# TensorE's expert loop: the turning back of the outputs moved ahead of the jump to the expert's code, and skipped before the first expert

## The chip, the cores and the metric

The kernel runs on one core of a Trainium2 chip. The metric is the device time of one launch in microseconds (us); less is better. The engines are called TensorE (PE in the profile, PEld its weight loads, PEldq what its sequencer does by itself: register operations, branches, waits), VectorE (DVE), ScalarE (ACT), GpSimd (POOL) and SyncE (SP, which issues DMAs).

## The reference, cut to what matters

A block of three parts on 2 x 1024 tokens of width 512: a mixture of experts, a gated mixer with a cumulative sum and a short convolution, and the same mixture of experts again. The change lies in the two mixtures.

```python
x = x + 0.5 * ffn(layernorm(x), gate_weight, wi, wo)
x = x + attn(layernorm(x), ...)
x = x + 0.5 * ffn(layernorm(x), gate_weight, wi, wo)

def ffn(inputs, gate_weight, wi, wo):        # 8 experts, 320 places each
    ...                                      # softmax, top 1, rank inside the expert
    dispatch = jnp.einsum('tec,th->ech', sec_mask, tokens)
    hmid = jax.nn.gelu(jnp.einsum('ech,ehi->eci', dispatch, wi), approximate=False)
    eout = jnp.einsum('eci,eih->ech', hmid, wo)
    return jnp.einsum('tec,ech->th', combine_weights, eout)
```

## The kernel before, in words

Each mixture (a `Layer`, n = 0 and 1) first computes where every token goes. Then the eight experts are worked through one after the other. Every matrix product is made of three: operands are split into a high and a low part in fp32r, and `product` and `onto` issue high x high, high x low and low x high (lines 1184 to 1186 and 1191 to 1193).

For an expert e TensorE first transposes its gathered and normalized tokens `dn`: `turn_tokens` (line 1355) is 12 transposes into four PSUM banks, `acc0`, `acc1`, `psH1` and `psH0`. ScalarE copies each bank to `dth`, VectorE subtracts and gives `dtl` (line 763), and counts `dt_lo` once for each of the four. The product with wi (`mm1`) goes into `psH`, the one with wo (`mm2`) is summed over the whole expert in the four banks `acc`. Those are cleared before by `clear_acc`, four tiny matmuls (line 1361), for which the third `dtl` must be there (`dt_lo` at 4e + 3), since the banks `acc0` and `acc1`, and `psH1` for what comes behind, hold turned tokens until then.

The output of an expert, `eoT` (copied by ScalarE from `acc`, line 660), is transposed back one expert later: `turn_out` (line 1399) turns 128 + 128 of its 320 columns into `psT0` and `psT1`, eight transposes, and `turn_rest` (line 1406) the last 64 into `psH1`, four transposes. VectorE then scales and adds to `rows` (line 1043), and GpSimd scatters these to memory. Before the first expert of a layer both functions run on an `eoT` that holds nothing of use, and their counts keep the semaphores in step. `eoT` is set to zero once by VectorE at the very start (line 917).

Of the kernel before, what the change touches and what calls it, by code (L numbers as in the profile page):

```python
# [32 lines left out]
DC = D // P  # L33
E, INTER = 8, 2048
# [45 lines left out]
def build_kernel(nc, x, wuT, wvT, wg1T, wg2T, small_in, wi, wo, out):  # L80
# [6 lines left out]
    with ExitStack() as ctx:  # L87
# [12 lines left out]
        def put(name, shape, dt):  # L100
            t = at(name, shape, dt, top[0])
            top[0] += size(shape, dt)
            return t
# [59 lines left out]
        eoT = put("eoT", [P, DC, CAP], F32)  # L163
# [586 lines left out]
        def _(dve):  # L750
            seq = [0]

            def then(ins):

                ins.then_inc(dve_seq, 1)
                seq[0] += 1
# [157 lines left out]
            for bank in (*acc[2:], *psH):  # L914
                ins = dve.memset(bank[:, 0:CAP], 0.0)
            ins.then_inc(banks_set, 1)
            then(dve.memset(eoT[:, :, :], 0.0))
            then(dve.memset(gates[:, :, :], 0.0))
            for e in range(E):
                then(dve.memset(digit[:, e:e + 1], float(2 ** (CODE * e))))  # L920
# [7 lines left out]
            for n, s in enumerate(layers):  # L928
# [28 lines left out]
                def wi_split(e, step, s=s):  # L957
                    k = (step // 2) % 2
                    dve.wait_ge(s.wi_hi, STEPS * e + step + 1)
                    lo(wil[:, step % 2, :, :], raw_wi[k][:, :, (step % 2) * HALF:(step % 2 + 1) * HALF],  # L960
                       wih[:, step % 2, :, :]).then_inc(s.wi_lo, 1)

                def wo_split(e, step, s=s):
                    k = (step // 2) % 2
                    dve.wait_ge(s.wo_hi, STEPS * e + step + 1)
                    lo(wol[:, step % 2, :, :], raw_wo[k][:, (step % 2) * ICS:(step % 2 + 1) * ICS, :],
                       woh[:, step % 2, :, :]).then_inc(s.wo_lo, 1)

                def tokens(e, c, s=s):

                    dve.wait_ge(s.dt_hi, DC * e + c + 1)
                    lo(dtl[:, c, :], TURNED[c][:, 0:CAP], dth[:, c, :]).then_inc(s.dt_lo, 1)
# [3 lines left out]
                def stage(e, h, a, sources, s=s, base=base):  # L976

                    for k in range(CHUNKS):
                        dve.wait_ge(gathered[1 - a][k], base + 16 * h + 16 * a + 16)
                    q = bass.ds(CHUNKS * e + CHUNKS, CHUNKS)  # L980
                    dve.tensor_copy(dst_now[:, 1 - a, :], dst[:, q])
                    dve.tensor_copy(facts_now[:, 1 - a], table[:, q, :]).then_inc(s.now_set, 1)  # L982
                    if sources:
                        dve.tensor_copy(src_now[:, a, :], src[:, bass.ds(CHUNKS * e + 2 * CHUNKS, CHUNKS)]
                                        ).then_inc(s.src_set, 1)
# [7 lines left out]
                def hidden_split(e, step, s=s):  # L993

                    k = step % 2
                    dve.wait_ge(s.gelu_done, ICS + ICS * (STEPS * e + step + 1))
                    if k == 0:
                        dve.wait_ge(s.mm2a_done, PAIRS * e + step // 2 + 1)
                    else:
                        dve.wait_ge(s.acc_done, DC * (PAIRS * e + step // 2 + 1))  # L1000
                    dve.tensor_copy(hth[:, k, :, :], gel[:, k, :, :]).then_inc(s.ht_hi, 1)  # L1001
                    dve.wait_ge(s.ht_hi, STEPS * e + step + 1)
                    lo(htl[:, k, :, :], gel[:, k, :, :], hth[:, k, :, :]).then_inc(s.ht_lo, 1)

                def mixer_weights(i):

                    if i == 0:
                        dve.wait_ge(g_hi, 2)
                        lo(wg1[1][:, :, :], raw_g1[:, :, :], wg1[0][:, :, :]).then_inc(g_lo, 1)
                        lo(wg2[1][:, :], raw_g2[:, :], wg2[0][:, :]).then_inc(g_lo, 1)  # L1010
                    for step in (2 * i, 2 * i + 1):
                        k, c = divmod(step, DC)
                        dve.wait_ge(uv_hi, step + 1)
                        w = (wu, wv)[k]
                        lo(w[1][:, c, :], raw_u[k][:, c, :], w[0][:, c, :]).then_inc(uv_lo, 1)

                def expert(h, side, last, sources, s=s):
                    e = 2 * h + side
                    for i in range(PAIRS):
                        a, b = 2 * i, 2 * i + 1  # L1020
                        wo_split(e, b)
                        hidden_split(e, a)
                        if not last or a + 2 < STEPS:
                            wi_split(e, a + 2)
                        hidden_split(e, b)
                        if not last or b + 2 < STEPS:
                            wi_split(e, b + 2)
                        if i == 1 and not last:
                            stage(e, h, side, sources)
                        if last and s is layers[0]:  # L1030
                            mixer_weights(i)
                        if not last or a + 2 < STEPS:
                            wo_split(e, a + 2)

                    if not last:
                        for c in range(DC):
                            tokens(e + 1, c)
                    dve.wait_ge(s.now_set, e + 1)
                    for i, (k, bank) in enumerate(HELD):
                        m = ROWS[k]  # L1040
                        dve.wait_ge(s.outT_done, e + 2)
                        out_rows = rows[side][0:m, k, :]
                        dve.scalar_tensor_tensor(out_rows, bank[0:m, :], facts_now[0:m, side, k, WEIGHT:WEIGHT + 1],  # L1043
                                                 out_rows, ALU.mult, ALU.add).then_inc(s.out_dve, 1)
# [93 lines left out]
                for g in range(GROUPS):  # L1138
                    more = g + 1 < GROUPS
# [40 lines left out]
        def _(pe):  # L1180
# [23 lines left out]

            codes = pe.alloc_register("codes")
            width = pe.alloc_register("width")
            visits = [[], []]
            marks = []
            pe.wait_ge(pool_const, 3)
# [9 lines left out]
            for n, s in enumerate(layers):  # L1219
# [138 lines left out]
                def clear_acc():  # L1358

                    for c in range(DC):  # L1360
                        pe.matmul(acc[c][:, 510:512], ones[:, :], ones[:, 0:2], start=True, stop=True)
# [27 lines left out]
                    if k == 0:  # L1389
                        ins.then_inc(s.mm2a_done, 1)  # L1390

                def turn_out(e, s=s):

                    pe.wait_ge(s.out_dve, 3 * e)
                    for c in range(DC):
                        pe.wait_ge(s.eoT_done, DC * e + c + 1)
                        for k, bank in HELD[1:]:
                            q, m = k * P, ROWS[k]
                            pe.transpose(bank[0:m, c * P:(c + 1) * P], eoT[:, c, q:q + m], ident[:, :])  # L1399

                def turn_rest(s=s):

                    k, bank = HELD[0]
                    q, m = k * P, ROWS[k]
                    for c in range(DC):
                        ins = pe.transpose(bank[0:m, c * P:(c + 1) * P], eoT[:, c, q:q + m], ident[:, :])
                    ins.then_inc(s.outT_done, 1)

                def expert(e, w, s=s):
                    pe.wait_ge(s.dt_lo, DC * e + 3)  # L1410
                    clear_acc()
                    turn_rest()
                    with pe.Fori(0, PAIRS) as i:
                        mm1(e, 2 * i, 0, w)
                        mm1(e, 2 * i + 1, 1, w)
                        mm2(e, 2 * i, 0, w)
                        mm2(e, 2 * i + 1, 1, w)
# [12 lines left out]
                pe.wait_ge(s.taken_done, 1)  # L1430
                pe.reg_load(codes, code[0:1, 0:1])
                pe.wait_ge(s.wi_lo, 1)
                pe.addr_align(BLOCK, offset=BLOCK - 2, max_nops=0)
                with pe.Fori(0, E) as e:
                    pe.wait_ge(s.dn_done, CHUNKS * e + CHUNKS)
                    for c in range(DC):
                        if c < 2:
                            pe.wait_ge(s.eoT_done, DC * e + c + 1)
                        turn_tokens(e, c)
                    turn_out(e)  # L1440
                    pe.reg_alu(width, codes, 2 ** CODE - 1, ALU.bitwise_and)
                    pe.reg_alu(codes, codes, CODE, ALU.logical_shift_right)
                    head = nc.cur_bb
                    dispatch("run")
                    nc.switch_bb(f"join_{n}", parent=head)
                    pe.addr_align(BLOCK, offset=BLOCK - 3, max_nops=0)
# [7 lines left out]
                        pe.addr_align(BLOCK, offset=BLOCK - 1, max_nops=0)  # L1454
                        pe.br(f"visited_{w}_{n}")
                nc.switch_bb(f"done_{n}", parent=over_bb)
                turn_out(E)
                turn_rest()

                if n == 1:  # L1460
                    break
# [72 lines left out]
                for g in range(GROUPS):  # L1534
                    more = g + 1 < GROUPS
# [89 lines left out]
```

## Time and profile before

| | |
|---|---|
| time, median of 3 runs | 1121.2 us (1119.05 to 1122.02) |
| the profiled execution's own time | 1119.05 us |
| its span, first to last instruction | 1117.3 us |
| TensorE's mean granted clock in it | 0.966 of full |
| TensorE matmul busy | 1049.7 us (94%) |
| VectorE busy | 722.1 us (65%) |
| ScalarE busy | 545.4 us (49%) |
| GpSimd busy | 148.0 us (13%) |

A boundary between two experts is the stretch from the last `mm2` matmul of one to the first `mm1` matmul of the next. There are 14 of them, seven in each layer, and two starts of a layer. They are called here by the expert that begins: 1 to 7 of the first layer, 1 to 7 of the second, and expert 0 for a start. The widths, by the shapes of line 1184, are 288, 304, 272, 240, 288, 240, 240, 256 in the first layer and 320, 240, 240, 240, 240, 240, 320, 320 in the second.

### The profile page before, as it was taken

How to read it: one execution, taken by the hardware profiler on the slowest of the kernel's cores; microseconds unless marked ns; L12 is line 12 of the kernel's file. 1: busy time of each engine (PE TensorE's matmuls, PEld its weight loads, DVE VectorE, ACT ScalarE, POOL GpSimd, SP SyncE). 2: the span in 40 equal slices, each digit the busy share in tenths (PEclk: the TensorE clock that was granted, in tenths of full speed). 3: DMA queues.
4: the chain of work that ended last, by engine and by line, in shares of the span. 5: the costliest groups of instructions: out<-in, count | busy, mean ns of one | idle time of the engine just before them, and what ended most of it. 6: DMA issues, size and time to landing. Idle time of an engine off the chain costs nothing.

```text
span 1117.3 us, 20930 instructions
## 1 busy us (share of the span) xinstructions
PE 1049.7 (94%) x7898; PEld 996.1 (89%) x7898; DVE 722.1 (65%) x1089; ACT 545.4 (49%) x853; POOL 148.0 (13%) x135
## 2 busy tenths in 40 slices
PE   8599999999999999399999995999999999999995
PEld 6599999999999999377777774999999999999995
DVE  7466556666676777378776774557767677665652
ACT  5345445655556565254243223445656656554441
POOL 2201102113020210100000013002112021130101
PEclk9599999999999999699999996999999999999998
DMA  8368636475555651400011017445475565654400
GB/s 304 103 253 297 229 114 230 146 254 195 195 202 188 239 187 63 165 10 1 1 39 37 2 49 269 156 143 211 177 250 212 204 215 195 233 203 149 171 38 24
DMA packets 83283, 177.43 MB, mean 159 GB/s; under 512 B 4192, under 2 KB 4704, under 8 KB 83168
## 3 DMA queue, kind: packets, MB, share of 16 engines
q1 hardware_dynamic: 75776, 153.13, 38.7%
q0 software_dynamic: 7168, 23.07, 5.7%
q8 instruction: 34, 0.56, 0.2%
q10 hardware_dynamic: 288, 0.52, 0.1%
q14 instruction: 17, 0.14, 0.0%
HBM read 162.04 MB, written 18.87 MB: 162 GB/s over the span
## 4 chain that ended last, share of the span: by engine, by line
PE 90%; DMA 2%; issue 2%; DVE 2%; ACT 1%; POOL 1%; POOLq 0%; SPq 0%; DVEq 0%; ACTq 0%
PE psH L1184 12%; PE psH L1186 12%; PE psH L1185 12%; PE acc L1193 11%; PE acc L1191 11%; PE acc L1192 11%; PE acc L1184 3%; PE acc L1186 3%; PE acc L1185 3%; PE psT L1399 1%; PE psT L1235 1%; PE psH L1307 1%; PE acc L1355 1%; PE psH L1355 1%; DMA rows<-out_x,src_now 1%
## 5 line engine op out<-in xcount | busy, mean ns | idle before, releaser
L1184 PE MATMUL psH<-dth,wih 128*128 128x240 f32 (+5 forms) x1024 | 295.4, 288 | 0.1
L1186 PE MATMUL psH<-dth,wil 128*128 128x240 f32 (+5 forms) x1024 | 294.2, 287 | 0.0
L1185 PE MATMUL psH<-dtl,wih 128*128 128x240 f32 (+5 forms) x1024 | 293.9, 287 | 0.0
L1193 PE MATMUL acc<-hth,wol 128*128 128x240 f32 (+5 forms) x1024 | 293.5, 287 | 0.0
L1191 PE MATMUL acc<-hth,woh 128*128 128x240 f32 (+5 forms) x1024 | 293.2, 286 | 0.0
L1192 PE MATMUL acc<-htl,woh 128*128 128x240 f32 (+5 forms) x1024 | 293.2, 286 | 0.0
L763 DVE TENSOR_TENSOR wol<-raw_wo,woh 128x1024 fp32r<-128x1024 f32 x128 | 155.6, 1222 | 140.3 <-ACT woh L594 140.3
L628 ACT ACTIVATE gel<-psH 128x320 f32<-128x320 f32 x256 | 111.8, 437 | 188.7 <-PE psH L1186 183.4
L594 ACT ACTIVATE woh<-raw_wo 128x1024 fp32r<-128x1024 f32 x128 | 134.2, 1056 | 126.4 <-PE acc L1193 126.4
L1184 PEld LDWEIGHTS psH<-dth,wih 128*128 128x128 f32 x1024 | 193.7, 189 | 0.6 <-ACT gel L628 0.2
L1186 PEld LDWEIGHTS psH<-dth,wil 128*128 128x128 f32 x1024 | 193.7, 189 | 0.0
L1185 PEld LDWEIGHTS psH<-dtl,wih 128*128 128x128 f32 x1024 | 193.7, 189 | 0.0
L1193 PEld LDWEIGHTS acc<-hth,wol 128*128 128x128 f32 x1024 | 193.0, 188 | 0.0
L1191 PEld LDWEIGHTS acc<-hth,woh 128*128 128x128 f32 x1024 | 193.0, 188 | 0.0
L1192 PEld LDWEIGHTS acc<-htl,woh 128*128 128x128 f32 x1024 | 193.0, 188 | 0.0
L763 DVE TENSOR_TENSOR wil<-raw_wi,wih 128x1024 fp32r<-128x1024 f32 x128 | 155.8, 1219 | 0.1
L583 ACT ACTIVATE wih<-raw_wi 128x1024 fp32r<-128x1024 f32 x128 | 134.6, 1053 | 1.4 <-DMA raw_wi<-in_wi 1.3
L1001 DVE CAST hth<-gel 128x640 fp32r<-128x640 f32 x128 | 63.3, 494 | 93.0 <-ACT gel L628 92.5
L763 DVE TENSOR_TENSOR htl<-gel,hth 128x640 fp32r<-128x640 f32 x128 | 105.7, 826 | 4.4
L498 POOL DMA_INDIRECT out_x<-rows,dst_now x24 | 35.7, 1488 | 326.2 <-DVE rows L1043 321.4
L498 POOL DMA_INDIRECT x<-rows,dst_now x24 | 35.3, 1470 | 322.3 <-DVE rows L1043 317.4
L611 ACT ACTIVATE dn<-rows,facts_now 128x512 f32<-128x512 f32 x48 | 38.9, 810 | 63.6 <-DVE facts_now L982 37.4
(189 smaller groups left out, 1158.6 us busy)
## 6 DMA issues: line engine op xcount, KB each, us to landing
raw_wi<-in_wi SPq DMA_DIRECT2D x64, 1024.0 KB, 5.1
raw_wo<-in_wo SPq DMA_DIRECT2D x64, 1024.0 KB, 5.4
out_x<-xt SPq DMA_DIRECT2D x4, 1024.0 KB, 5.1
xt<-in_x SPq DMA_DIRECT2D x6, 512.0 KB, 8.2
xt<-x SPq DMA_DIRECT2D x3, 1024.0 KB, 9.7
raw_u<-in_wuT SPq DMA_DIRECT2D x1, 1024.0 KB, 10.3
raw_u<-in_wvT SPq DMA_DIRECT2D x1, 1024.0 KB, 12.4
xt<-x SPq DMA_DIRECT2D x4, 256.0 KB, 3.4
```

Of the source, the lines that this page charges most:

```text
L498: pool.indirect_dma_start(target[:, :], bass.IndirectOffsetOnAxis(ap=dst_now[0:m, a, k:k + 1], axis=0), rows[a][0:m, k, :], None).then_inc ...
L583: act.activation(wih[:, step % 2, :, :], raw_wi[k][:, :, (step % 2) * HALF:(step % 2 + 1) * HALF], copy).then_inc(s.wi_hi, 1)
L594: act.activation(woh[:, step % 2, :, :], raw_wo[k][:, (step % 2) * ICS:(step % 2 + 1) * ICS, :], copy).then_inc(s.wo_hi, 1)
L628: act.activation(gel[:, step % 2, j, :], psH[j][:, 0:CAP], ACT.Gelu).then_inc(s.gelu_done, 1)
L763: return dve.tensor_tensor(out, full, hi.bitcast(F32), ALU.subtract)
L1001: dve.tensor_copy(hth[:, k, :, :], gel[:, k, :, :]).then_inc(s.ht_hi, 1)
L1184: pe.matmul(out, lh, rh, start=first, stop=False)
L1185: pe.matmul(out, lh, rl, start=False, stop=False)
L1186: return pe.matmul(out, ll, rh, start=False, stop=last)
L1191: pe.matmul(out, lh, rh, start=False, stop=False, skip_group_check=True)
L1192: pe.matmul(out, lh, rl, start=False, stop=False, skip_group_check=True)
L1193: return pe.matmul(out, ll, rh, start=False, stop=False, skip_group_check=True)
```

## The change

It does four things. (1) `clear_acc` and `turn_rest` leave the code of the widths and stand in the loop over e, behind the eight transposes of `turn_out` and ahead of the two register operations and the ladder. The wait for the third `dtl` moves with them. (2) A new register, `later`, is 0 for expert 0 and 1 behind it. With 0 the loop only waits for the third `dtl` and clears the banks: none of the 12 transposes of `eoT` is made, and `outT_done` isn't counted. With 1 it does what the kernel before did. (3) VectorE waits for `outT_done` one lower, since it counts one fewer. (4) The setting of `eoT` to zero goes.

```diff
-            then(dve.memset(eoT[:, :, :], 0.0))
...
-                        dve.wait_ge(s.outT_done, e + 2)
+                        dve.wait_ge(s.outT_done, e + 1)
...
+            later = pe.alloc_register("later")
...
-                def turn_out(e, s=s):
+                def turn_out(e, more=True, s=s):
 
                     pe.wait_ge(s.out_dve, 3 * e)
                     for c in range(DC):
@@
                         for k, bank in HELD[1:]:
                             q, m = k * P, ROWS[k]
                             pe.transpose(bank[0:m, c * P:(c + 1) * P], eoT[:, c, q:q + m], ident[:, :])
-
-                def turn_rest(s=s):
-
+                    if more:
+                        pe.wait_ge(s.dt_lo, DC * e + 3)
+                        clear_acc()
                     k, bank = HELD[0]
                     q, m = k * P, ROWS[k]
                     for c in range(DC):
                         ins = pe.transpose(bank[0:m, c * P:(c + 1) * P], eoT[:, c, q:q + m], ident[:, :])
                     ins.then_inc(s.outT_done, 1)
 
-                def expert(e, w, s=s):
-                    pe.wait_ge(s.dt_lo, DC * e + 3)
-                    clear_acc()
-                    turn_rest()
+                def expert(e, w):
                     with pe.Fori(0, PAIRS) as i:
...
+                pe.reg_mov(later, 0)
                 pe.addr_align(BLOCK, offset=BLOCK - 2, max_nops=0)
                 with pe.Fori(0, E) as e:
...
-                    turn_out(e)
+                    with pe.If_lt(later, 1):
+                        pe.wait_ge(s.dt_lo, 3)
+                        clear_acc()
+                    with pe.Else():
+                        turn_out(e)
+                    pe.reg_mov(later, 1)
                     pe.reg_alu(width, codes, 2 ** CODE - 1, ALU.bitwise_and)
                     pe.reg_alu(codes, codes, CODE, ALU.logical_shift_right)
...
-                turn_out(E)
-                turn_rest()
+                turn_out(E, False)
```

## Rows read from the trace of the kernel before

**Rows 1.** The page: TensorE's busy time, and the chain's shares.

```profile
PE 1049.7 (94%) x7898; PEld 996.1 (89%) x7898; DVE 722.1 (65%) x1089; ACT 545.4 (49%) x853; POOL 148.0 (13%) x135
...
PE 90%; DMA 2%; issue 2%; DVE 2%; ACT 1%; POOL 1%; POOLq 0%; SPq 0%; DVEq 0%; ACTq 0%
```

**Rows 2.** Timeline at expert 1, first layer: start us, us, engine, line, count, [idle before].

```profile
104.42 0.88 DVE L763 TENSOR_TENSOR dtl<-psH,dth 128x320 fp32r<-128x320 f32 x2
104.95 0.17 PEld L1361 LDWEIGHTS acc<-ones 128*128 128x128 bf16 x4 [0.23 <-DVE dtl L763]
...
105.43 0.19 PEld L1184 LDWEIGHTS psH<-dth,wih 128*128 128x128 f32 x1
```

**Rows 3.** Sequencer by line, experts 0 and 1: ns min/median/max, first and last start.

```profile
L1413 PEldq MOVE  x1: 34/34/34, 50.5 to 50.5; - x1
...
L1441 PEldq ALU_OP  x1: 36/36/36, 103.3 to 103.3; - x1
L1426 PEldq COMPARE_BRANCH  x5: 64/69/207, 103.5 to 104.1; - x5
L1413 PEldq MOVE  x1: 29/29/29, 105.0 to 105.0; - x1
```

**Rows 4.** Sequencer by line: ladders of 240, 288, 320 and 272 columns.

```profile
L1426 PEldq COMPARE_BRANCH  x1: 213/213/213, 313.8 to 313.8; - x1
L1441 PEldq ALU_OP  x1: 36/36/36, 313.6 to 313.6; - x1
...
L1426 PEldq COMPARE_BRANCH  x4: 64/76/331, 260.3 to 260.8; - x4
...
L1441 PEldq ALU_OP  x1: 36/36/36, 984.7 to 984.7; - x1
L1428 PEldq COMPARE_BRANCH  x1: 169/169/169, 985.6 to 985.6; - x1
...
L1426 PEldq COMPARE_BRANCH  x3: 69/82/3562, 159.3 to 159.6; - x3
```

**Rows 5.** Timeline at expert 2, first layer: VectorE's last two dtl, and TensorE.

```profile
160.25 0.88 DVE L763 TENSOR_TENSOR dtl<-psH,dth 128x320 fp32r<-128x320 f32 x2
163.26 0.17 PEld L1361 LDWEIGHTS acc<-ones 128*128 128x128 bf16 x4 [2.71 <-issue]
```

**Rows 6.** Windows: from:to us, length, busy by engine (x count), PEclk granted clock, DMA.

```profile
47.20:51.40 4.20, 4.17 (x20) 4.17 (x21) 1.97 (x4) 2.62 (x6) 2.84 (x3) 0.50 0.91 320
163.50:167.00 3.50, 3.50 (x20) 3.47 (x19) 2.97 (x4) 0.40 (x1) 1.41 (x1) 0.58 0.02 5
472.50:478.00 5.50, 5.47 (x20) 4.52 (x21) 2.08 (x3) 4.23 (x8) 0.00 (x0) 0.50 0.58 220
478.00:481.50 3.50, 2.11 (x9) 1.29 (x7) 1.29 (x3) 1.69 (x3) 0.00 (x0) 0.98 0.00 0
672.50:676.00 3.50, 2.06 (x40) 1.86 (x41) 2.44 (x17) 1.51 (x2) 0.00 (x0) 1.00 0.99 316
```

**Rows 7.** Timeline at expert 0 of the first layer.

```profile
49.63 1.72 PEld L1399 LDWEIGHTS psT<-ident,eoT 128*128 128x128 f32 x8
...
49.92 1.13 DVE L763 TENSOR_TENSOR dtl<-psH,dth 128x320 fp32r<-128x320 f32 x2
...
51.34 0.32 PEld L1361 LDWEIGHTS acc<-ones 128*128 128x128 bf16 x4
...
51.95 0.19 PEld L1184 LDWEIGHTS psH<-dth,wih 128*128 128x128 f32 x1
```

**Rows 8.** Timeline at expert 0 of the second layer: the third dtl, and the first mm1.

```profile
695.89 0.49 DVE L763 TENSOR_TENSOR dtl<-psH,dth 128x320 fp32r<-128x320 f32 x1
...
697.50 0.19 PEld L1184 LDWEIGHTS psH<-dth,wih 128*128 128x128 f32 x1
```

**Rows 9.** Timeline of VectorE at the kernel's start.

```profile
2.55 1.12 DVE L917 MEMSET eoT<- 128x1280 f32 x1 [0.26 <-issue]
...
5.73 0.19 DVE L924 TENSOR_TENSOR gates<-small,acc 128x32 f32<-128x32 f32 x1 [1.79 <-PE acc L1216]
```

## The prediction

> **What bounds the kernel now.** I read the page first. TensorE's matmuls are busy for 1049.7 of the span's 1117.3 us, and the chain of work that ended last lies on TensorE for 90% [rows 1]. So whatever holds TensorE up at an expert's boundary is paid in full, and whatever another engine saves there is worth nothing by itself. Next I read the timeline at each boundary, because the change lies there alone. At expert 1 the eight transposes of `turn_out` are done, TensorE is idle for 0.23 us for the third `dtl`, then clears, turns the rest, and loads the first weights of `mm1` at 105.43 [rows 2]. The other warm boundaries look the same to within 0.02 us, except expert 2.
>
> The timeline shows no branches, so the third view is the sequencer's own instructions, line by line. At expert 1 the first register operation of the ladder starts at 103.3, its five comparisons run from 103.5 to 104.1 and the last takes 0.21; then nothing until the `MOVE` that opens the inner loop, at 105.0 [rows 3]. The third `dtl` ends at 104.42 + 0.49 = 104.91 (one of them takes 0.49 [rows 8]; the two of the row overlap). So the ladder is free today: it runs while the sequencer would otherwise wait for `dtl`. And the sequencer stands at that wait; it doesn't run on past it. Expert 0 shows this best: the third `dtl` ends at 49.92 + 0.49 = 50.41, the `MOVE` comes at 50.5 [rows 3], although TensorE only reaches the clearing at 51.34 [rows 7]. Three times the `MOVE` follows the third `dtl` by about 0.08 us. From the `MOVE` to the first weight load of `mm1` are 0.45 us (105.0 to 105.43) of register operations and waits; the array needs about as long for clearing and turning (104.95 to 105.43). The boundary is therefore balanced: anything put on the sequencer behind the wait comes out at `mm1`.
>
> **The change, part by part.** The wait for the third `dtl` now stands ahead of the ladder. Behind it, one after the other, come: the pushes of 8 instructions (inside the 0.08 us), `reg_mov`, the two register operations, the ladder, the inner loop's opening, `mm1`.
>
> *The ladder, 14 boundaries.* Its price is from the start of line 1441 to the end of the last branch [rows 4]. For 240 columns 313.8 + 0.21 - 313.6 = 0.41; for 288 260.8 + 0.33 - 260.3 = 0.83 and the 0.2 of the two register operations ahead of it (103.3 to 103.5), 1.03; for 304 104.1 + 0.21 - 103.3 = 1.01 [rows 3]; for 320 985.6 + 0.17 - 984.7 = 1.07. For 272, 159.6 - 159.1 = 0.5 up to the jump and a normal jump of 0.21, so 0.7; for 256 I take 0.7 too, between 240 and 288 and near 272. Seven boundaries in the first layer: 1.01 + 0.7 + 0.41 + 1.03 + 0.41 + 0.41 + 0.7 = 4.7. In the second five of 240 and two of 320: 2.05 + 2.14 = 4.2. A last jump can take 0.33 instead of 0.21, as at 288; for others like it I allow 0.3 more. Together 9.2 us. Of this nothing is hidden, by the balance above; at most the 0.02 us of slack.
>
> The Trainium skill ("Advanced Engine Details and Errata", Control Flow Timing) puts a compare-and-branch at about 108 ns and an unconditional one at about 51 ns. By it the 32 comparisons behind these 14 boundaries and two jumps would be an estimated 3.6 us, and with the two register operations unpriced the ladder would come out far cheaper; the trace has steps of 0.12 to 0.2 and a last jump of 0.21 to 0.35, and it decides.
>
> *`reg_mov` and the joint.* A register operation takes a step of 0.1 us (line 1441 to the first comparison is 0.2 for two [rows 3]), and a branch leaves about 0.03 before the next: 14 x 0.13 = 1.8.
>
> *The end of the Else part.* It may need a jump to where both parts meet. The trace has none; the nearest row is line 1428 with 0.17 [rows 4]. So 0 to 14 x 0.17 = 2.4; I take the middle, 1.2. The comparison for `later` is ahead of `turn_out`, where the sequencer waits for ScalarE's last `eoT` anyway: nothing.
>
> *Expert 0, without the transposes.* TensorE saves 12 transposes in each layer, some 2 us of a slow clock in the first. But `mm1` can't start before the sequencer's chain is through: third `dtl` 50.41 + 0.08 + 0.1 + ladder 0.9 + 0.03 + 0.45 = 51.97, against 51.95 today [rows 7]: nothing. In the second layer (320 columns) 696.38 + 0.08 + 0.1 + 1.07 + 0.03 + 0.45 = 698.1, against 697.50 [rows 8]: 0.6 lost. With the joint's jump 0.2 more for both. Bounds: 0.4 and 1.2.
>
> *The clock at expert 0.* TensorE comes to each layer's first expert at the lower level, 1.2 GHz: from 47.2 to 51.4 it works without a break at a granted 0.50, and then the clock is full, just before `mm1` starts [rows 6]. The transposes that the change takes out are the second half of that work. Without them TensorE works from 47.2 to about 49.8, is idle for 2 us, and the heavy matmuls start cold. How long they stay so: the stretch of unbroken work ahead of the rise was 4.2 us here and 5.5 us at 472.5 to 478 [rows 6]. Half of it is lost, 2.1 to 2.8; it was 3.4 us behind expert 2's gap (0.58 granted over 3.5 us), 1.7. I take 1.9 for each layer, 3.8 together; bounds 0 (the clock rises in spite of the gap) and 5.6.
>
> *Expert 2 of the first layer.* Its ladder's last jump took 3.56 us: the code for 272 wasn't there and was fetched. 1.15 us of that is hidden today, since the jump starts at 159.6 and the third `dtl` is ready at 160.25 + 0.49 = 160.74; the rest is in the idle 2.71 [rows 4, 5]. Afterwards the jump starts at 160.74 + 0.08 + 0.1 + 0.5 = 161.4 and ends at 165.0, where it ends by 163.26 today: 1.7, of which 0.8 is counted in the ladder and joint, so 0.9 more. The clock fell behind that gap and was half for some 3.4 us; behind one of 3.9 it may stay so for as long again: 0 to 1.7, I take 0.9.
>
> *The clock at the other boundaries.* Each gets an idle gap of 0.5 to 1.2 us beside today's 0.23. With 2.11 of 3.5 us busy the clock stayed full at 478, and with 2.06 it fell behind 676 [rows 6]; a boundary for 304 or 320 columns leaves about as much. A fall costs 1.7. Four boundaries are that wide: 0 to 6.8, and I take 0.5, as all but the widest stay well above.
>
> *VectorE's memset.* 1.12 us are gone, but VectorE then waits 1.79 us for TensorE's first product [rows 9]: nothing; with less than that wait it would be worth its 1.12 at most. VectorE's wait for `outT_done` one lower is the same event as before, and its adding to `rows` is hidden behind `mm1` as now.
>
> Sum: 9.2 + 1.8 + 1.2 + 0.6 + 0.2 + 3.8 + 0.9 + 0.9 + 0.5 = 19.1 us. On the profiled execution's own 1119.05 (its span of 1117.3 and 1.75 around it) that is 1138.2. The median of the runs shown lies 2.15 higher; I add part of that and say 1139.
>
> **The rivals.** (a) *The sequencer isn't held.* If a waiting transpose is handed to the array's queue and the sequencer goes on, the ladder stays hidden. Then only expert 0 changes: `mm1` follows the fourth `dtl` (49.92 + 1.13 = 51.05, and 0.1 [rows 7]), 0.8 earlier in the first layer and at most as much in the second, and without or with the 3.8 of the clock the time is 1117.5 to 1121.3: no change. It decides if at every boundary the first branch of line 1426 starts ahead of the third `dtl`. Against it speaks that the `MOVE` comes behind the wait at all boundaries. The Trainium skill ("Perfetto Trace Analysis", per-instruction lifecycle) says for TensorE just what this rival needs: the wait is served in a queue behind the sequencer, which is ready for the next instruction after the push. By that rule the trace would have the `MOVE` of expert 1 near 104.4; it has it at 105.0 [rows 3]. 6 in 100.
>
> (b) *The fetch of expert 2 goes away.* The loop's code gets longer and the widths' shorter, and which blocks are at hand could change. But both still fit in a block each, and the order in which blocks are entered is the same. Then expert 2 saves 1.7 instead of losing 1.7, and 2.6 of clock: 1138.2 - 6.0 = 1132. 10 in 100.
>
> (c) *More falls of the clock or more fetches.* A fetch costs 3.4 and its fall of the clock 1.7; two of them, or six falls beyond those counted, give 1148; a fall at all 14 boundaries 1160. For it: the boundaries come close to the stretch behind which the clock fell. Against: TensorE worked through 478 to 481.5 with as much idle time at full clock. 8 in 100.
>
> My forecast, then, has 76 in 100.
>
> **How the numbers follow.** The likeliest is 1139. With the low ends of the unknown costs (no joint's jump, no loss of clock at expert 0) it is 1119.05 + 9.2 + 1.8 + 0.4 + 0.9 = 1131.4; with the high ones (2.4, 1.2, 5.6, 1.7, 3.4) 1119.05 + 9.2 + 1.8 + 2.4 + 1.2 + 5.6 + 0.9 + 1.7 + 3.4 = 1145.3, and 2 more for the median. With (b) and most of (c) the range is 1130 to 1148. About 0.3% is what a measurement of this kernel can tell from no change. Faster needs both (a) and (b): 2 in 100. Within 0.3% is the rest of (a): 4. Slower is all else: 94.
>
> **What would show it.** In the profile of the changed kernel the ladder's first branch should start about 0.3 us behind the third `dtl`, and `mm1`'s first weight load about 1.0 us behind it for 240 columns and 1.7 for 320, where it is 0.53 now. TensorE should show a new idle gap at each boundary behind the rest's transposes, put down to issue. The clock should be half for some us behind the start of `mm1` in both first experts. The long jump should stand at expert 2 again. Wrong would be the prediction if those gaps are missing (a), if the long jump is gone or is there more than once (b, c), or if the second layer's 240s lose more than the ladder's 0.41 and about 0.2.

## The result

The changed kernel takes 1138.18 us (median; 1137.5 to 1140.88), the kernel before 1121.2 us (1119.05 to 1122.02). The ratio is 1.0157, with a 95% interval of 1.0142 to 1.0174: slower by 17 us. The profiled execution took 1136.17 us, with a span of 1134.3, against 1119.05 and 1117.3 before. The forecast was 1139 in a range of 1130 to 1148. All ratios here are of fast executions; of all executions below two were slow, one of 5902.66 us (the filler) and one of 2693.16 us (the second entry into the code).

The page of the changed kernel, its span, TensorE's time and the chain's shares, beside [rows 1]:

```profile
span 1134.3 us, 20909 instructions
...
PE 1053.2 (93%) x7874; PEld 995.7 (88%) x7874; DVE 721.8 (64%) x1088; ACT 545.7 (48%) x853; POOL 147.5 (13%) x135
...
PE 89%; issue 3%; DMA 2%; DVE 2%; ACT 2%; POOL 1%; POOLq 0%; SPq 0%; DVEq 0%; ACTq 0%
```

TensorE makes 24 matmuls fewer (the 12 transposes of each layer's expert 0) and is none the less busy for 3.5 us longer, which is the clock; "issue" in the chain has gone from 2% to 3%. The list of TensorE's waits names the place (waiter, what released it: us in total, times, longest):

```profile
PE psH L1183 <- issue: 14.5, 16, 3.8
```

Sixteen waits, one for each expert, ahead of the first `mm1` matmul, released by nothing but the sequencer. The kernel before has no such row. Line 1183 is `product`'s first matmul, 1184 before: most lines on TensorE stand one to three higher or lower now.

The timeline at expert 1 of the first layer, beside [rows 2]:

```profile
105.57 0.91 PEld L1399 LDWEIGHTS psT<-ident,eoT 128*128 128x128 f32 x8
...
106.17 0.88 DVE L763 TENSOR_TENSOR dtl<-psH,dth 128x320 fp32r<-128x320 f32 x2
...
106.70 0.17 PEld L1361 LDWEIGHTS acc<-ones 128*128 128x128 bf16 x4 [0.23 <-DVE dtl L763]
...
106.80 0.36 PEld L1406 LDWEIGHTS psH<-ident,eoT 128*64 128x64 f32 x4
...
108.25 0.19 PEld L1183 LDWEIGHTS psH<-dth,wih 128*128 128x128 f32 x1 [1.09 <-issue]
```

And the sequencer's own instructions there, beside [rows 3]:

```profile
L1443 PEldq MOVE  x1: 29/29/29, 106.7 to 106.7; - x1
...
L1444 PEldq ALU_OP  x1: 36/36/36, 106.8 to 106.8; - x1
...
L1423 PEldq COMPARE_BRANCH  x5: 64/69/207, 107.0 to 107.5; - x5
...
L1410 PEldq MOVE  x1: 29/29/29, 107.8 to 107.8; - x1
```

Up to the clearing nothing has moved: it comes 2.47 us behind the first transpose of tokens in both kernels (104.24 to 106.70 here), with the same 0.23 us of waiting for the third `dtl`. Then the old order was clearing, `MOVE` of the inner loop, `mm1`; the new one has the move of `later` (106.7), two register operations, five comparisons and only then the loop's `MOVE` at 107.8. TensorE's weight loads for the four transposes are over by 107.16, and the weight-load side is idle for 1.09 us; on the matmul side, where the sum of 14.5 us is taken, the gap is 0.83.

The distance from the first weight load of `turn_tokens` (line 1355) to the first one of `mm1`, read from the two timelines, in us:

| expert | 0 | 1 | 2 | 3 | 4 | 5 | 6 | 7 |
|---|---|---|---|---|---|---|---|---|
| layer 1, columns | 288 | 304 | 272 | 240 | 288 | 240 | 240 | 256 |
| before | 4.72 | 2.94 | 5.44 | 2.93 | 2.90 | 2.94 | 2.90 | 2.90 |
| after | 5.24 | 4.01 | 7.01 | 3.62 | 4.04 | 3.52 | 3.50 | 3.72 |
| layer 2, columns | 320 | 240 | 240 | 240 | 240 | 240 | 320 | 320 |
| before | 4.30 | 2.96 | 2.91 | 2.90 | 2.90 | 2.90 | 2.90 | 2.96 |
| after | 5.37 | 3.66 | 3.47 | 3.50 | 3.51 | 3.47 | 4.09 | 4.12 |

The 14 boundaries grew by 11.8 us, the two starts by 1.6. Behind the starts the first expert itself took 1.5 us longer in the first layer and 2.6 in the second, at the same number of matmuls. That is 17.6; the rest of the span gave back 0.6 (0.3 ahead of the first expert and 0.7 in the mixer gained, 0.4 lost inside the other experts), which makes the 17.0 between the spans.

The 1.5 and 2.6 are the clock, as windows of the changed kernel show (columns as in [rows 6]; the granted clock is the third number from the end):

```profile
49.80:51.90 2.10, 0.25 (x4) 0.16 (x4) 1.50 (x3) 2.10 (x3) 0.69 (x1) 1.00 1.00 381
...
53.20:56.60 3.40, 3.40 (x17) 3.40 (x16) 0.35 (x1) 0.44 (x1) 0.00 (x0) 0.50 0.46 166
...
700.80:706.00 5.20, 3.08 (x16) 2.61 (x16) 2.88 (x5) 3.64 (x6) 2.83 (x3) 0.50 0.93 317
706.10:712.10 6.00, 5.92 (x22) 5.93 (x23) 1.34 (x2) 0.44 (x1) 0.00 (x0) 0.51 0.66 201
```

In the first layer the clock had just risen, TensorE did almost nothing for 2.1 us, and the clock fell again for 3.4 us in the middle of `mm1`. In the second it never rose ahead of `mm1` and stayed at 1.2 GHz for the first 6 us of it.

### The profile page after: what moved, and what is told of

The parts are those of the page before. It is cut to its first block, busy times and chain, and to the rows that moved or that the text cites. A ratio compares the mean times of both kernels' runs of the same rounds, so it can differ in the third digit from the quotient of the medians.

```text
span 1134.3 us, 20909 instructions
## 1 busy us (share of the span) xinstructions
PE 1053.2 (93%) x7874; PEld 995.7 (88%) x7874; DVE 721.8 (64%) x1088; ACT 545.7 (48%) x853; POOL 147.5 (13%) x135
## 4 chain that ended last, share of the span: by engine, by line
PE 89%; issue 3%; DMA 2%; DVE 2%; ACT 2%; POOL 1%; POOLq 0%; SPq 0%; DVEq 0%; ACTq 0%
PE psH L1183 13%; PE psH L1184 12%; PE psH L1185 12%; PE acc L1191 11%; PE acc L1192 11%; PE acc L1190 11%; PE acc L1183 3%; PE acc L1184 3%; PE acc L1185 3%; PE psT L1235 1%; PE psT L1399 1%; PE psH L1307 1%; PE acc L1355 1%; PE psH L1355 1%; DMA rows<-out_x,src_now 1%
## 5 line engine op out<-in xcount | busy, mean ns | idle before, releaser
L1183 PE MATMUL psH<-dth,wih 128*128 128x240 f32 (+5 forms) x1024 | 297.4, 290 | 15.2 <-issue 14.5
```

Of the source, the lines that this page charges most:

```text
L1183: pe.matmul(out, lh, rh, start=first, stop=False)
```

## The experiments

They ran on three chips, four on each; which chip the first comparison ran on isn't known. There the kernel before took 1125.9 to 1128.3 us and scattered more. So two things are read: the ratio to the kernel before on the same chip, and, from one profiled execution of each kernel, the distances at the boundaries, which hardly differ from chip to chip. No profile of the kernel before was taken on these chips; where its behaviour there is spoken of, it is read from kernels that keep its boundaries.

**Hoisting alone.** The changed kernel without `later`, without If and Else and with the memset back.

```diff
-                    with pe.If_lt(later, 1):
-                        pe.wait_ge(s.dt_lo, 3)
-                        clear_acc()
-                    with pe.Else():
-                        turn_out(e)
-                    pe.reg_mov(later, 1)
+                    turn_out(e)
```

> One half of the change alone: clearing and the last four transposes stand ahead of the ladder at every expert, and nothing is skipped at expert 0 (no register later). Theory (the sequencer is held at the wait for the third dtl, so what stands behind it is paid in full): the 14 boundaries cost what the changed kernel's cost, 11.8 us, less a register move of 0.1 each, so 10.4; expert 0 costs 0 in the first layer and 0.5 in the second, and its clock rises ahead of mm1 as in the kernel before. Together 10.9 us, 1132 us. Rival (the loss comes from the skipping at expert 0 and its If and Else): no change, 1121 us.

The distances at the 14 boundaries grew by 10.55 us in all, at expert 0 by 0.09 and 0.69, and both first experts ran as fast as before: the distances are the expected ones to 0.2. The ratio is not: 1.0052 (1.0034 to 1.007), 1134.75 against 1128.28 us, some 6 us where 11 were due. The list of TensorE's waits has both the price and what came off:

```profile
PE psH L1184 <- issue: 10.3, 15, 4.0
...
PE psH L1184 <- ACT gel L628: 1.5, 2, 0.9
```

The second row, waits for gelu, is not in the list of the kernel before on the first chip. What it means came out of the next runs.

**Skipping alone**, on the kernel before: the eight transposes of `turn_out` are left out at expert 0, all else stays.

```diff
-                    turn_out(e)
+                    with pe.If_lt(first, 1):
+                        turn_out(e)
+                    pe.reg_mov(first, 0)
                     pe.reg_alu(width, codes, 2 ** CODE - 1, ALU.bitwise_and)
```

> The other half alone, on the kernel before: the eight transposes of turn_out are left out at expert 0, all else stays where it was (the last four transposes are still made at expert 0, and the ladder stays ahead of the wait). Theory: mm1 of expert 0 then follows the fourth dtl, 0.8 us earlier in the first layer and 0.35 in the second, but its matmuls run at the lower clock for some us, which costs 2 to 4.2; the 14 boundaries are unchanged. Together 1 to 3 us slower, 1122 to 1124 us, and the granted clock is half for some us behind the start of mm1 in both layers. Rival (the clock doesn't hang on these transposes): 1.2 us faster, 1120 us.

1126.39 against 1128.28 us, ratio 0.9984 (0.9967 to 1.0001). `mm1` of expert 0 came 0.82 and 0.31 us earlier, as expected, and 13 of the 14 boundaries stayed within 0.01 (expert 2, with the fetch, came 0.32 later). The clock cost little here: it rose to full at 50.3 us in the first layer, just as `mm1` started and TensorE had no gap behind it, and 1.3 us behind the start of `mm1` in the second, where the first expert took 0.6 us longer. The window of the first 1.7 us from there, columns as above:

```profile
50.30:52.00 1.70, 1.70 (x15) 1.70 (x14) 1.25 (x2) 1.36 (x2) 0.00 (x0) 1.00 0.83 289
```

The theory's 1 to 3 us slower lie outside the interval, and what was to be lost by the clock, 2 to 4.2, was 0.6. The rival's 1.2 us faster lie inside it: with the last four transposes left in their place, the eight others were hardly missed. And the waits for gelu are there again, in the list of TensorE's waits (us in total, times, longest):

```profile
PE psH L1184 <- ACT gel L628: 7.3, 6, 1.9
```

**More sequencer work behind the wait and ahead of it.** Two pairs. In the first, four more moves of the constant into `later`, behind the wait in the changed kernel and ahead of it in the kernel before.

> The changed kernel with the register move of later made five times instead of once, behind the wait for the third dtl and ahead of the ladder. Theory: each move costs a step of 0.1 us at each of 16 experts, 4 x 16 x 0.1 = 6.4 us on top of 1138.2, so 1144.6 us. Rival (the sequencer has slack there, and the loss is the array's or the clock's): 1138 us as without.

> The kernel before with the same four register moves between turn_out and the ladder, ahead of the wait for the third dtl. Theory: the ladder ends 0.55 us or more ahead of that wait's end, and four moves are 0.4 us, so nothing: 1121 us. Rival (a register operation costs TensorE its 0.1 us wherever it stands): 6.4 us, 1127.6 us.

These tell nothing on their question: the traces show none of the added moves (16 moves of `later` in the first kernel, one for each expert, and none in the second), so they weren't in the program that ran. They are a second look at the two kernels on a slower chip: 1141.39 us (ratio 1.0111, 1.0081 to 1.0141) and 1129.71 (1.0012, 0.9995 to 1.0029). The first has the changed kernel's distances again (12.3 us more at the 14 boundaries, 0.4 of the difference at expert 2 with its fetch), but its clock cost nothing at the first start and 2.5 us at the second, where the first look had 1.5 and 2.6.

In the second pair the extra work is five waits for semaphores that were reached long ago. In the trace they are two instructions for each expert, not five, and those start 0.11 us apart.

```diff
+                    for done in (s.taken_done, s.rank_done, s.tabled, s.oh_done, s.lgT_copied):
+                        pe.wait_ge(done, 1)
                     pe.reg_alu(width, codes, 2 ** CODE - 1, ALU.bitwise_and)
```

> The changed kernel with five waits for semaphores that have long been reached put between the last four transposes and the ladder, at every expert. Theory: the sequencer serves each in 0.05 to 0.1 us and mm1 starts that much later at all 16 experts, 4 to 8 us on top of the changed kernel. Rival (the sequencer has slack there): nothing.

> The kernel before with the same five waits between turn_out and its ladder, ahead of the wait for the third dtl. Theory: the ladder of the widest code ends 0.55 us ahead of that wait's end, so the five waits are hidden at all boundaries, or cost 0.1 at those for 320 columns: nothing. Rival: the same 4 to 8 us as behind the wait.

The two instructions at expert 1, behind the wait:

```profile
L1445 PEldq EVENT_SEMAPHORE  x2: 51/51/51, 107.7 to 107.8; - x2
```

Behind the wait each distance grew by some 0.21 us over the changed kernel's (for 240 columns, at experts 2 to 5 of the second layer, 3.68 to 3.72 instead of 3.47 to 3.51; for 320 columns 4.30 instead of 4.09), and by 0.55 at expert 2, whose fetch took longer: 3.7 us over 16 experts, a little less than the 4 to 8 expected. Ahead of it 13 boundaries stayed within 0.01 us of the kernel before. Expert 2 came 0.42 later, where the fetch took 3.77 instead of 3.56 us, and the two starts 0.38 and 0.22 later, which tells nothing: over the five kernels that keep the old order and all transposes the start lies 4.1 to 5.1 us behind the first transpose in the first layer and 4.3 to 5.1 in the second. The sum of TensorE's waits for the sequencer in the first of the two went from 14.5 to:

```profile
PE psH L1183 <- issue: 18.3, 16, 4.4
```

Times: 1142.8 us (ratio 1.0127, 1.0095 to 1.0158) and 1126.41 (0.9988, 0.9969 to 1.0007). At the boundaries the same instructions are paid or free by the side of the wait on which they stand.

**Work for the clock.** The changed kernel with eight transposes of the identity at expert 0, which nothing reads.

```diff
                     with pe.If_lt(later, 1):
+                        for c in range(DC):
+                            for _, bank in HELD[1:]:
+                                pe.transpose(bank[:, c * P:(c + 1) * P], ident[:, :], ident[:, :])
                         pe.wait_ge(s.dt_lo, 3)
```

> The changed kernel, with eight transposes of the identity put back at expert 0 ahead of the clearing, as work for the array alone: nothing reads them. Theory: the start of mm1 at expert 0 stays where the changed kernel has it (5.2 and 5.4 us behind the first transpose of tokens), as the sequencer sets it, but the clock rises ahead of or shortly behind it in both layers, so that the 4.2 us that the changed kernel's profile lost there by the clock come back, or most of them: 1134 to 1136 us where the changed kernel takes 1138. Rival (the clock's fall is set by the idle time ahead of mm1 alone, which stays): as the changed kernel.

`mm1` started where the changed kernel starts it (5.22 and 5.36 us behind the first transpose, against 5.24 and 5.37), and the first experts then took 0.00 us longer than before in both layers, where the changed kernel took 1.5 and 2.6. The windows over the same stretches:

```profile
51.90:56.60 4.70, 4.08 (x34) 4.00 (x33) 2.26 (x2) 1.64 (x4) 0.00 (x0) 0.99 0.46 145
...
706.00:712.00 6.00, 5.16 (x36) 5.05 (x35) 3.12 (x4) 2.71 (x4) 0.67 (x1) 0.89 0.58 208
```

The clock is full when `mm1` starts (in the second layer it rose at 707.3, and `mm1` starts at 708.5), and stays so. So TensorE's missing work ahead of `mm1` is what the clock's loss comes from. The rival isn't settled by this, though, since the idle time didn't stay: the eight transposes fill most of it. TensorE's first weight load of `mm1` at expert 0, first in the changed kernel, then with the filler:

```profile
52.15 0.19 PEld L1183 LDWEIGHTS psH<-dth,wih 128*128 128x128 f32 x1 [1.84 <-issue]
...
52.74 0.19 PEld L1183 LDWEIGHTS psH<-dth,wih 128*128 128x128 f32 x1 [0.70 <-issue]
```

Whether the shorter gap or the longer work ahead of it keeps the clock, no run separates. And in the first layer alone the 0.00 would prove little, as the changed kernel lost nothing there either in the profile of the repeated moves; in the second it lost 1.3 to 2.6 in all its profiles. The time was 1136.07 us, ratio 1.0059 (1.0039 to 1.008). The changed kernel itself didn't run on this chip; the kernel with the five waits, less their 3.7 us, makes an estimated 1139, some 3 us more than with the filler.

**The fetch of expert 2.** The kernel before, with one more jump into each width's code meant to be made from the loop's own block, ahead of the first layer's loop.

> The kernel before, with one more jump into each of the six widths' code from the block of the loop itself, once in the first layer, while TensorE waits for the first gathered rows. Theory: the code for 272 columns is then at hand at expert 2, so its jump takes 0.2 instead of 3.6 us, mm1 starts 2.5 us earlier there, and the clock doesn't fall behind it, 1.7 us: 4.2 us faster than the kernel before, unless the jumps themselves hold up expert 0. Rival (the blocks at hand are fewer than eight, so the code is pushed out again): no change, or a second long jump elsewhere, up to 3.5 us slower.

1127.48 against 1128.03 us, ratio 0.9988 (0.9969 to 1.0006), no change. The long jump stood at expert 2 as always, the longest of the 41 branches:

```profile
L1426 PEldq COMPARE_BRANCH  x41: 64/78/3680, 48.2 to 1060.5; - x41
```

But the run tells nothing on theory and rival, because the extra jumps weren't made. The trace has not one instruction of the added lines (1435 and 1463) and 208 branches on TensorE's sequencer, just as many as the kernel before. Between the last entry into a width's code and the loop stands one branch, into the aligned block, and at once the load of `codes`. It is a further look at the kernel before, no more:

```profile
L1431 PEldq COMPARE_BRANCH  x1: 396/396/396, 45.6 to 45.6; - x1
...
L1438 PEldq TENSOR_LOAD <-code x2: 319/402/484, 46.1 to 696.5; - x2
```

Whether a second entry would keep the code for 272 columns at hand, and why it alone is gone by then, stays open.

**Where part of the loss goes on a slower chip.** The waits for gelu were 7.3, 6.4, 4.8 and 4.3 us in the four kernels above with the old boundaries (skipping alone, the repeated moves ahead, the second entry into each width's code, the waits ahead), and 1.5, 1.7, 2.0 and 1.7 in the four with the ladder behind the wait (hoisting alone, the repeated moves behind, the filler, the waits behind). Each is of one profiled execution; the first and the third of these took 4 and 7 us more than their kernel's median. At the first of those with old boundaries, ScalarE stood behind VectorE, and VectorE behind its copy for the next expert (`stage`, line 981), which waits for the gathered rows. That wait in the kernel with the repeated moves, old boundaries, on the slower chip, then in the kernel before on the first chip, then in hoisting alone:

```profile
DVE dst_now L981 <- DMA rows<-out_x,src_now: 10.5, 5, 3.4
...
DVE dst_now L981 <- DMA rows<-in_x,src_now: 7.0, 3, 2.9
```

```profile
DVE dst_now L981 <- DMA rows<-out_x,src_now: 5.6, 5, 1.4
...
DVE dst_now L981 <- DMA rows<-in_x,src_now: 2.6, 3, 0.9
```

```profile
DVE dst_now L981 <- DMA rows<-out_x,src_now: 7.6, 5, 2.3
...
DVE dst_now L981 <- DMA rows<-in_x,src_now: 2.7, 3, 1.1
```

The median gather took 5.9 and 6.3 us from issue to landing in the first of these and 5.2 and 5.3 in the second. In the third, on the same chip as the first, it was 5.0 and 5.9, and in the changed kernel in the first comparison 4.7 and 5.7: so it differs between kernels on one chip too, and not by the chip alone. The chain scatter, gather, `stage` starts when the outputs have been turned back, which the change leaves where it is; `mm1` and all behind it comes 0.6 to 1.2 us later. So the theory: a later `mm1` gives this chain room, and part of the loss pays for waits that would have come. The last four runs test that, on one chip. The move in both kernels is:

```diff
-                        if i == 1 and not last:
-                            stage(e, h, side, sources)
                         if last and s is layers[0]:
                             mixer_weights(i)
                         if not last or a + 2 < STEPS:
                             wo_split(e, a + 2)
+                        if i == 1 and not last:
+                            stage(e, h, side, sources)
```

and on ScalarE its first `norm_rows` likewise behind `wo_split(e, a + 2)`.

> The changed kernel itself, unchanged, on the chip of the next three. Theory: where the gathers and scatters of rows take longer (the kernel before takes 1128 instead of 1121 us), the kernel before loses 4 to 7 us in waits of VectorE for gathered rows, which hold up TensorE through ScalarE's gelu; the changed kernel starts mm1 later by 0.6 to 1.2 us at each boundary, while the scatter and gather start at the same time, so it loses only 1 to 2 us there. Its ratio to the kernel before is then 1.010 to 1.012 and not 1.0157. Rival (the loss is the same everywhere): 1.015 to 1.017.

> The kernel before, with VectorE's wait for the gathered rows (and ScalarE's first normalization behind it) moved behind the next split of wo, so that it stands in nobody's way some 2 us longer. Theory: TensorE's waits for gelu at the later steps go away: 4 to 6 us faster than the kernel before on a chip where that takes 1128, 0 to 1 on one where it takes 1121. Rival (the wait moves on to the normalized rows or to the next gather, or those waits have another cause): no change or slower.

> The changed kernel with the same move of VectorE's wait. Theory: it has only 1 to 2 us of such waits to lose, so it gains 1 to 2 us over the changed kernel, and stands 14 to 18 us behind the kernel before with the move: the whole price of the change is seen once nothing absorbs it. Rival: it gains as much as the kernel before does, and the distance stays as in the pair without the move.

> The kernel before with that move and with the eight transposes of turn_out left out at expert 0: the candidate that keeps what the change saves without what it costs. Theory: mm1 of expert 0 starts 0.8 and 0.3 us earlier, and the clock costs 0 to 2.6 us in each layer, by where its rise falls: between 1 us faster and 4 us slower than the kernel with the move alone. Rival: 1.1 us faster each time.

| kernel | median us | ratio to before | waits for gelu, us |
|---|---|---|---|
| changed | 1140.83 | 1.0138 (1.0119 to 1.0157) | 0.3 |
| before, late stage | 1121.33 | 0.9960 (0.9945 to 0.9974) | none |
| changed, late stage | 1137.85 | 1.0112 (1.0093 to 1.0131) | none |
| before, late stage, skipping alone | 1118.55 | 0.9945 (0.9926 to 0.9964) | 0.8 |

The kernel before took 1125.89 us on this chip. The late stage took 4.6 us off it and 3.0 off the changed kernel, and with nothing left to absorb it the price of the change is 16.5 us, where it was 14.9 without the move. What is shown is that the late stage takes time off the kernel before (its interval lies below 1) and that no wait for gelu is left with it. The rest is not: the intervals of the changed kernel with and without the move overlap, 16.5 and 14.9 differ by less than the intervals allow, and 1.0138 (1.0119 to 1.0157) lies between the theory's 1.010 to 1.012 and the rival's 1.015 to 1.017. Nor is it shown that slow gathers make a chip slower: in these four traces the median gather took 4.6 to 5.6 us, no more than in the first comparison, though the kernel before took 1125.89 here. The last kernel is faster than both the kernel before and the changed one. Of its 7.3 us, 4.6 are the late stage's; the intervals of the two overlap, so that skipping adds to it isn't shown by the times. Its distances at expert 0 are 0.20 and 0.52 us shorter than with the late stage alone, and its clock fell at neither start.

## Why the prediction was right

Step by step, forecast and measured, in us:

| step | forecast | measured |
|---|---|---|
| 14 boundaries: ladder, move, jump out of Else, expert 2's fetch | 9.2 + 1.8 + 1.2 + 0.9 = 13.1 | 11.8 |
| start of `mm1` at expert 0, both layers | 0.8 | 1.6 |
| clock at expert 0, both layers | 3.8 | 4.2 (1.5 + 2.6) |
| clock behind expert 2, and elsewhere | 0.9 + 0.5 | 0 |
| memset | 0 | not above 0.3 |
| rest of the span | 0 | -0.5 |
| sum | 19.1 | 17.1 (1136.17 - 1119.05) |

The total is nearer than its terms. Forecast less measured they are 1.3, -0.8, -0.4, 1.4 and 0.5 us off, which partly cancel, and the 0.8 added for the median met a median 2.0 above the profiled execution. That the forecast of 1139 came within 1 us of 1138.18 is luck in part; that it is 17 us slower, and why, is not.

*The sequencer is held at the wait.* This carried the forecast, and all of it held: no boundary overlapped, the waits with issue appeared at all 16, and the paired waits, behind and ahead, show it by themselves. Rival (a) is out, and with it, for this kernel, the picture of a wait served behind a sequencer that has gone on. Whether it stands at the waiting instruction itself or at the matmuls that follow it (in every kernel some stand between the wait and the next register operation) no run separates.

*The ladder.* The prices read from the kernel before were right to a tenth: 0.91 now for 304 columns and 0.40 for 240, by the same reckoning, against 1.01 and 0.41 (unrounded, the ladder for 304 took 0.96 in the kernel before, and the one for 288 also 0.96 and not 1.03). One term was too large: a jump at the end of Else isn't there (the move of `later` comes at 106.7, with the clearing). That jump is at the end of the If part instead, at expert 0, and takes more than the 0.17 of the nearest row:

```profile
L1438 PEldq COMPARE_BRANCH  x1: 405/405/405, 50.2 to 50.2; - x1
```

In the second layer it took 0.35. So expert 0 lost 0.51 and 1.07 instead of 0.1 and 0.7, 1.6 in all, which is more than the upper bound of 1.2 that the prediction gave.

*The clock at expert 0.* Mechanism and sum were right; the filler run shows that the work missing ahead of `mm1` is the cause. But the size isn't a property of the kernel alone: 1.5 and 2.6, 0 and 2.5, 1.5 and 1.3 in three profiles of the same program, and 0 and 0.6, then 0 and 0, where the last four transposes stay. That is about the width that the bounds of 0 to 5.6 gave it.

*The other falls of the clock.* The forecast allowed 1.4 us and none came. With idle gaps of 0.6 to 1.2 us on the weight-load side (0.3 to 1.0 for matmuls) at each warm boundary the clock stayed full in the changed kernel, and behind the longer gap of expert 2 it fell for 3.4 us, as it had behind the shorter.

*The fetch.* Rivals (b) and (c) didn't come: one long jump in the ladders, at the same place. Its branch took 3.44 us there, and the distance grew by 1.57 where 1.7 were forecast.

*What the prediction didn't see* is that the ratio may differ from chip to chip. In the first comparison nothing stood behind the later `mm1`; elsewhere kernels with the old boundaries waited for gathered rows, and the ratio was 1.0138 and 1.0111 for the same change. Only the second of these has an interval (1.0081 to 1.0141) clear of the first comparison's.

## What to carry to other kernels

Before an instruction with a wait is moved ahead of register operations and branches, look at what the sequencer did during that wait: work of its own that was free there is paid for behind it, here to the tenth of a microsecond. Work for TensorE that computes nothing of use can still pay by the clock it keeps up; take it out only where what follows doesn't start cold, or look at the granted clock behind it. And when a delay costs less in the times than on the timeline, look for a chain that the delay gave room: here moving the waiting copy gained 4.6 us, more than the 1 us or so that skipping at expert 0 could save. And look in the trace for the instructions that an experiment adds: two of the experiments here, the repeated moves and the second entry, ran without them.

## What the runs showed of the hardware that was not expected

The profile's own records of the sequencer price control flow well: a comparison that goes on to the next takes a step of 0.12 to 0.14 us in most ladders, a register operation 0.1, a ladder's last jump into another block 0.17 to 0.35, the jump out of the If part 0.35 and 0.41, and an instruction that waits for semaphores long reached 0.11. The one ladder's jump to code that had to be fetched took 3.3 to 3.9 us on the sequencer, at expert 2 of the first layer in all 14 profiles, though that code had been entered once before the loop. A rise of the clock that has just come can be lost at once: full at 49.8 us, 2.1 us of almost no work, half from 53.2 to 56.6.
